# Hard graph attention on one core: a new order on ScalarE and VectorE, one copy of the turned keys, and the normalised rows written by GpSimd

## The chip, the core and the metric

The kernel runs on one core of a Trainium2 chip, as one launch. The metric is the device time in microseconds (us). Its engines are TensorE (PE, with its weight loads PEld), VectorE (DVE), ScalarE (ACT), GpSimd (POOL) and SyncE (SP, which only issues DMAs here). Each engine runs its own list of instructions in order and waits on semaphores that the others raise. ps_... tiles lie in PSUM, the others in SBUF; PE writes into PSUM only.

## The reference

There are 4096 nodes with 256 features, and a random 0/1 matrix adj of 4096 x 4096, dense in its first rows and columns and thinner towards the last ones. For each of 8 heads, only the neighbours with the highest score count, and each with 1/8:

```python
Q, K, V = (x @ WQ.T), (x @ WK.T), (x @ WV.T)          # split into 8 heads of 32
attn = einsum('hqd,hkd->hqk', Q, K) * SCALING + (Q @ we.T + be)
attn = softmax(attn + where(adj > 0, 0.0, -inf))
hard = (attn == max(attn, axis=-1, keepdims=True)) / HEADS
y = layernorm(x + einsum('hqk,hkd->hqd', hard, V), eps=1e-5)
```

## The kernel before, in words

**Prologue.** The projections are made for all nodes. The queries stay in SBUF (q_t); keys and values, the latter in three bf16 parts, go to a table in DRAM (kv_table) of 640 words a row.

**Items.** The queries are taken in groups of 32 (GQ), four groups to a tile of 128 rows, 32 tiles in all. A group needs only the nodes that any of its queries has as a neighbour. Those are gathered 372 at a time (three chunks of 124); such a gather is an *item*. A group has between 1 and 12 items; the run makes some 200. Four items make a *turn* (RING = 4, b = 0 to 3 in the code), and one body for a turn is run in a loop on each engine. SP plans the turns ahead and writes flags for each: fe_on (a new tile of adj is cast and packed), fin_on (its lists are finished), te_on (a tile of results is finished: te_done is its number).

**One item m, engine by engine.** ACT makes `reached` from the ends of the item (owners, line 621). PE multiplies it with the packed lists (planes_of, line 1199). DVE finds the neighbours and their masks from that (pick, line 926: hit, hit_vals, picks, bits). POOL gathers the rows by three indirect DMAs into kv[m % 8] (gather, line 527) and copies the queries (queries, line 522). ACT turns the bits into `masked` (masks, line 654). PE transposes the keys, both halves of four heads, into the two banks of ps_both[m % 2] (keys_across, line 1241), and raises pe_kt[h] for each half; ACT copies each half into k_t (keys, line 660) and raises act_kt[h]. PE makes the scores into the same two banks (scores, line 1215). DVE takes their minimum (tops, line 948: best), then the running minimum (minus_top), and then whether the old one still holds (keep). ACT compares the scores with minus_top (hards, line 664: two instructions). PE transposes the result (hards_across, line 1232), ACT copies it back (hard_rows, line 650: hard_t), PE multiplies with the values into ps_o (values, line 1249), and DVE adds it onto o_all, which is first multiplied by keep (merge, line 962: two instructions).

**The order in a step b.** The engines are in different items at the same time:

- PE: planes_of(b+4), scores(b+1), values(b-1), hards_across(b), keys_across(b+2).
- ACT: masks(b+2), hard_rows(b), owners(b+5), keys(b+2), then hards(b+1). The casts of adj (joined, line 605) stand at b = 0 (quarter 0, behind hards), b = 1 (quarter 1 ahead of hards, 2 behind it) and b = 2 (quarter 3, ahead of hards).
- DVE: pick(b+4), tops(b+1), merge(b-1).
- POOL: queries(b+2), gather(b+3).

PE writes into ps_o for item b only when merge(b-1) has read it, and it writes hard_t's source again only when act_hard has come. scores waits for act_kt[1], the second half alone.

**A finished tile** (te_on). At b = 1 DVE turns o_all (turn_rows, line 972) behind pick and ahead of tops, and PE multiplies it back into ps_y (rows_back, line 1263). At b = 2 DVE adds x and takes mean and variance (norm_stats, line 978) between pick and tops. ACT takes the root (row_std, line 671: std) at b = 2, behind keys and cast_quarter(3) and ahead of hards. DVE then makes rstd and y_out (norm_rows, line 990) behind tops and ahead of merge. SP stores y_out when dve_row is raised (line 479). The last tile is finished after the loop.

The lines that the change and the steps of the prediction touch: 237 to 238 (semaphores of the keys), 475 to 480 (store), 509 to 576 (POOL), 654 to 709 (ACT), 948 to 960 and 990 to 996 and 1099 to 1104 (DVE), 1218 and 1241 to 1247 (PE).

Of the kernel before, what the change touches and what calls it, by code (L numbers as in the profile page):

```python
# [38 lines left out]
def hard_attention(nc, x, adj, wq, wk, wv, we, be, out):  # L39
# [24 lines left out]
    with ExitStack() as ctx:  # L64
# [161 lines left out]
        def item_sem(name, ahead):  # L226
# [10 lines left out]
        pe_kt = [item_sem(f"pe_kt{h}", 2) for h in range(HALVES)]  # L237
        act_kt = [item_sem(f"act_kt{h}", 1) for h in range(HALVES)]
# [6 lines left out]
        dve_turned, pe_y, dve_y, act_std, dve_row = (  # L245
            sem("dve_turned"), sem("pe_y"), sem("dve_y"), sem("act_std"), sem("dve_row"))
# [111 lines left out]
        def _(sp):  # L358
# [116 lines left out]
            def rows(t, row, last):  # L475
# [3 lines left out]
                sp.wait_ge(dve_row, t + 1)  # L479
# [30 lines left out]
        def _(pool):  # L510
# [7 lines left out]
            r = registers(pool, ("n", "left", "g", "next", "more", "due", "at_turn", "col") + tuple(places("q", 1)),  # L518
# [27 lines left out]
            def load_more():  # L546
                at = pool.snap(r["at_turn"], min_val=0, max_val=TURNS - 1)
                pool.reg_load([r["more"]], turn_flags[0:1, bass.ds(at, 1), FLAGS.index("more"):])
# [7 lines left out]
            def turn(first):  # L556
                for b in range(RING):
# [4 lines left out]
                    if b == 2:  # L562
                        plan_made(pool, r)
                        load_places(pool, r, QUERY, places("q", 1))
                        load_more()
                        step()

# [7 lines left out]
            run_turns(pool, r, [lambda: turn(0), lambda: turn(RING)])  # L575
            twice = (pool.snap(r["n"]) - BASE) >> 3
# [6 lines left out]
        def _(act):  # L583
            for s in act_kt + [act_reached, act_masked, act_hard, act_hard_t]:
                act.sem_inc(s, credit(s))
# [74 lines left out]
            def keys(m, due, h):  # L660
                act.wait_ge(pe_kt[h], due(pe_kt[h]))
                act.copy(k_t[m % 2][:, h, :], ps_s[m % 2][h][:, 0:SLOTS]).then_inc(act_kt[h], 1)  # L662
# [13 lines left out]
            for m in range(2):  # L676
                masks(m, for_item(m))
                for h in range(HALVES):
                    keys(m, for_item(m), h)
            hards(0, for_item(0))  # L680

            def turn():
# [4 lines left out]
                for b in range(RING):  # L687
                    masks(b + 2, for_loop(act, r, 2))
                    hard_rows(b, for_loop(act, r, 0))
                    owners(b + 5, for_loop(act, r, 5), f"ahead{b + 5}")  # L690
                    for h in range(HALVES):
                        keys(b + 2, for_loop(act, r, 2), h)
# [5 lines left out]
                    if b == 2:  # L698
                        cast_quarter(3)
                        with rows_due(act, r):  # L700
                            row_std(tile_of(act, r, "te_done"))
                    if b == 3:
                        take_plan()
# [698 lines left out]
```

## Time and profile before

| | us |
|---|---|
| median of 3 runs | 1316.35 (1309.31 to 1316.83) |
| the profiled execution | 1317.37 |
| its span, first to last instruction | 1315.6 |
| of it, the stretch taken as the loop of items in the rows below | 240 to 1310 |

The profiled execution is 1.8 us beyond its span, and 1.0 us above the median. Busy times are of instructions that compute; register work, waits and branches are not busy. The mean granted TensorE clock is 0.918 of full speed.

### The profile page before, as it was taken

The numbers are of one execution on the slowest core, as the hardware profiler recorded it, in microseconds if no ns is written. First come the engines' busy times: TensorE is split into PE (matmuls) and PEld (weight loads), VectorE is DVE, ScalarE is ACT, GpSimd is POOL, SyncE is SP. The second block draws the span as 40 slices with busy tenths as digits, with TensorE's granted clock in tenths as the row PEclk, the third lists the DMA queues.
The fourth block names the chain that finished last, engine by engine and source line by source line (L and its number), as shares of the span: only waits on it lengthen the run. The fifth ranks groups of instructions, "written<-read, shape, count | busy, mean of one in ns | idle before, by whom it ended". The sixth has DMA issues, their size and how long they took to land.

```text
span 1315.6 us, 51593 instructions
## 1 busy us (share of the span) xinstructions
PE 951.6 (72%) x14758; PEld 616.6 (47%) x14759; DVE 929.0 (71%) x2616; ACT 892.0 (68%) x1688; POOL 632.8 (48%) x820
## 2 busy tenths in 40 slices
PE   4787648777777778777787777777777777777771
PEld 2343325454544555455454545455445545455540
DVE  5444536777878777777787777777777777778880
ACT  1523347778777787777877877877777777766770
POOL 0000065675656566555565555554554455445650
PEclk9988877999999998989999899989998989989995
DMA  4634468677687787678777878778878787756770
GB/s 155 214 128 160 145 201 279 196 231 255 197 263 217 243 253 234 215 242 266 248 207 231 268 226 262 252 230 272 257 235 258 248 251 254 254 180 194 212 213 4
DMA packets 89522, 291.06 MB, mean 221 GB/s; under 512 B 16984, under 2 KB 30040, under 8 KB 89496
## 3 DMA queue, kind: packets, MB, share of 16 engines
q0 software_dynamic: 48720, 199.60, 49.5%
q1 hardware_dynamic: 40776, 91.15, 20.4%
q8 instruction: 12, 0.20, 0.1%
q14 instruction: 14, 0.11, 0.0%
HBM read 275.98 MB, written 14.71 MB: 221 GB/s over the span
## 4 chain that ended last, share of the span: by engine, by line
DVE 26%; PE 25%; issue 20%; ACT 15%; DVEq 7%; DMA 3%; ACTq 2%; SPq 1%; POOL 1%; POOLq 0%
DVE best L951 6%; ACT joined L605 5%; PE ps_both L1222 4%; ACT k_t L662 4%; PE ps_both L1154 4%; DVE picks L941 3%; PE ps_h L1237 3%; PE ps_o L1257 3%; DVE hit_vals L934 3%; PE ps_r L1267 3%; DVE hit L928 2%; PE ps_both L1227 2%; ACT hard L667 2%; PE ps_both L1144 2%; DVE o_all L968 2%
## 5 line engine op out<-in xcount | busy, mean ns | idle before, releaser
L532 POOL DMA_INDIRECT kv<-kv_table,picks x309 | 294.9, 954 | 231.3 <-DVE picks L941 127.6
L532 POOL DMA_INDIRECT early<-kv_table,picks x300 | 286.2, 954 | 246.0 <-DVE picks L941 131.6
L652 ACT ACTIVATE hard_t<-ps_h 128x768 bf16<-128x768 bf16 x200 | 162.0, 810 | 233.1 <-PE ps_h L1237 227.4
L667 ACT ACTIVATE hard<-ps_both,minus_top 128x384 bf16<-128x384 f32 x402 | 214.1, 594 | 32.9 <-DVE minus_top L955 30.3
L1222 PE MATMUL ps_both<-k_t,q_now 32*32 32x384 f32 x3216 | 192.6, 534 | 32.1 <-ACT k_t L662 29.0
L951 DVE TENSOR_REDUCE best<-ps_both 128x2 f32<-128x768 f32 x201 | 190.7, 949 | 28.0 <-PE ps_both L1227 17.8
L1207 PE MATMUL ps_x<-pay,reached 128*128 x1224 | 120.2, 233 | 99.6 <-ACT reached L624 93.3
L662 ACT COPY k_t<-ps_both 128x384 f32<-128x384 f32 x404 | 171.6, 479 | 14.4 <-PE ps_both L1245 14.3
L968 DVE SCALAR_TENSOR_TENSOR o_all<-o_all,keep,ps_o 128x96 f32 x400 | 107.7, 311 | 61.8 <-issue 26.5
L1207 PEld LDWEIGHTS ps_x<-pay,reached 128*128 128x128 bf16 x1224 | 83.7, 102 | 137.5 <-ACT reached L624 128.0
L605 ACT ACTIVATE joined<-adj_in,minus_half 128x1024 bf16<-128x1024 int32 x128 | 147.9, 1164 | 0.0
L1227 PEld LDWEIGHTS ps_both<-mask_of,masked 128*128 128x128 bf16 x1206 | 72.9, 102 | 140.9 <-issue 140.9
L525 POOL COPY q_now<-q_t 128x64 f32 x202 | 50.4, 249 | 167.4 <-issue 164.3
L656 ACT ACTIVATE masked<-bits,one 124x384 bf16<-124x384 uint32 x202 | 127.6, 631 | 1.4 <-issue 1.4
L624 ACT ACTIVATE reached<-iota_h,edge_of 128x384 bf16<-128x384 f16 x205 | 124.1, 605 | 1.3 <-DVE pay L906 0.8
L1227 PE MATMUL ps_both<-mask_of,masked 128*128 128x128 bf16 x1206 | 109.4, 231 | 0.0
L1237 PE MATMUL ps_h<-ident_b,hard 128*128 128x128 bf16 x1200 | 107.6, 229 | 0.0
L941 DVE TENSOR_REDUCE picks<-hit_vals 128x9 uint32<-128x288 f32 x204 | 92.7, 455 | 15.1 <-DVE hit_vals L934 9.8
L934 DVE TENSOR_TENSOR hit_vals<-ps_x,hit 128x288 f32<-128x288 f32 x204 | 93.3, 458 | 7.0
L1245 PE MATMUL ps_both<-ident_f,kv 128*128 128x128 f32 x612 | 87.6, 281 | 12.0 <-DMA kv<-kv_table,picks 12.0
L1245 PE MATMUL ps_both<-ident_f,early 128*128 128x128 f32 x600 | 90.5, 291 | 1.6 <-DMA early<-kv_table,picks 1.6
L928 DVE SCALAR_TENSOR_TENSOR hit<-ps_x,slot_of,slot 128x96 f32<-128x96 f32 x204 | 64.0, 314 | 31.5 <-issue 16.1
(145 smaller groups left out, 1309.5 us busy)
## 6 DMA issues: line engine op xcount, KB each, us to landing
adj_in<-in_adj SPq DMA_DIRECT2D x128, 512.0 KB, 5.7
kv_table<-early SPq DMA_DIRECT2D x32, 320.0 KB, 2.4
kv<-kv_table,picks POOLq DMA_INDIRECT x309
early<-kv_table,picks POOLq DMA_INDIRECT x300
early<-in_x SPq DMA_DIRECT2D x8, 512.0 KB, 6.8
x_row<-in_x SPq DMA_DIRECT2D x32, 128.0 KB
out<-y_out SPq DMA_DIRECT2D x32, 128.0 KB
plan<-places_of SPq DMA_DIRECT2D x212, 0.0 KB
```

Source lines behind the costliest of these rows:

```text
L532: pool.indirect_dma_start(kv[m % KVS][:, c, :], None, kv_table, bass.IndirectOffsetOnAxis(ap=picks[m % RING][:, c, 2:3], axis=0)).then_inc ...
L605: act.activation(joined[:, i * QW:(i + 1) * QW], adj_in[:, i * QW:(i + 1) * QW], ACT.Sign, bias=minus_half[:]).then_inc(act_cast, 1)
L652: act.activation(hard_t[m % 2][:], hard_rows_t, ACT.Copy, bias=1.0).then_inc(act_hard_t, 1)
L662: act.copy(k_t[m % 2][:, h, :], ps_s[m % 2][h][:, 0:SLOTS]).then_inc(act_kt[h], 1)
L667: done = act.activation(hard[m % 2][:, h, :], ps_s[m % 2][h][:, 0:SLOTS], ACT.Sign, bias=minus_top[m % 2][:, h:h + 1], scale=-1.0)
L951: dve.tensor_reduce(best[:], ps_both[m % 2][:, :, 0:SLOTS], AX.X, ALU.min).then_inc(dve_best, 1)
L968: done = dve.scalar_tensor_tensor(out=o_run, in0=o_run, scalar=keep[m % RING][:, h:h + 1], in1=ps_o[:, h * width:(h + 1) * width], op0=ALU ...
L1207: mm = pe.matmul(ps_x[:, c * P:(c + 1) * P], reached[m % 2][:, c * P:(c + 1) * P], pay[:].rearrange("p g i v -> p (g i v)") [:, bass.ds(va ...
L1222: pe.matmul(ps_s[m % 2][h][to:to + GQ, 0:SLOTS], q_now[m % RING][head:head + HD, h, :], k_t[m % 2][head:head + HD, h, :], start=True, stop ...
L1227: mm = pe.matmul(bank[:, c * P:(c + 1) * P], masked[m % RING][:, c, :, :].rearrange("p h q -> p (h q)"), mask_of[:], start=False, stop=(c ...
L1237: mm = pe.transpose(hard_rows_t[:, at:at + P], hard[m % 2][:, h, c * P:(c + 1) * P], ident_b[:])
L1245: mm = pe.transpose(ps_s[m % 2][h][:, c * P:(c + 1) * P], kv[m % KVS][:, c, h * P:(h + 1) * P], ident_f[:])
```

## The change

1. ACT, in each step: owners(b+5) now comes first, then masks(b+2), hard_rows(b), keys(b+2). Before it was masks, hard_rows, owners, keys.
2. The keys of both halves are one copy of 128x768 out of both banks, with one semaphore on either side (pe_kt, act_kt) where there were two.
3. ACT, at b = 2: row_std ahead of cast_quarter(3).
4. DVE, tops: keep is worked out first, by comparing max(old, cap) with best (is_le), and so needs no wait for minus_top; then minus_top, with no wait of its own.
5. DVE, at b = 2: merge ahead of norm_rows.
6. y_out is written by POOL (normal_rows) and no more by DVE. POOL does it at b = 3 behind gather, waits there for st_out and for the reciprocal (dve_norm), and raises pool_row, for which the store on SP and the next norm_stats wait. POOL reads one more flag for it (te_on).

```diff
@@ -234,16 +234,15 @@
         q_made = item_sem("q_made", 1)
-        pe_kt = [item_sem(f"pe_kt{h}", 2) for h in range(HALVES)]
-        act_kt = [item_sem(f"act_kt{h}", 1) for h in range(HALVES)]
+        pe_kt, act_kt = item_sem("pe_kt", 2), item_sem("act_kt", 1)
         pe_score = [item_sem(f"pe_score{h}", 1) for h in range(HALVES)]
...
 
-        dve_turned, pe_y, dve_y, act_std, dve_row = (
-            sem("dve_turned"), sem("pe_y"), sem("dve_y"), sem("act_std"), sem("dve_row"))
+        dve_turned, pe_y, dve_y, act_std, pool_row = (
+            sem("dve_turned"), sem("pe_y"), sem("dve_y"), sem("act_std"), sem("pool_row"))
         dve_norm = sem("dve_norm")
@@ -476,7 +475,7 @@
                     sp.dma_start(x_row[:], x[bass.ds(row + P, P), :]).then_inc(ld_row, 16)
-                sp.wait_ge(dve_row, t + 1)
+                sp.wait_ge(pool_row, t + 2)
                 sp.dma_start(out[bass.ds(row, P), :], y_out[:]).then_inc(st_out, 16)
@@ -515,7 +514,8 @@
             pool.sem_inc(q_made, credit(q_made))
-            r = registers(pool, ("n", "left", "g", "next", "more", "due", "at_turn", "col") + tuple(places("q", 1)),
+            pool.sem_inc(pool_row, 1)
+            r = registers(pool, ("n", "left", "g", "next", "more", "due", "at_turn", "col", "te_on", "te_now", "te_done") + tuple(places("q", 1)),
                           n=BASE, left=1, due=PLANNED)
@@ -545,7 +545,13 @@
                 at = pool.snap(r["at_turn"], min_val=0, max_val=TURNS - 1)
-                pool.reg_load([r["more"]], turn_flags[0:1, bass.ds(at, 1), FLAGS.index("more"):])
+                pool.reg_load([r["te_on"], r["more"]], turn_flags[0:1, bass.ds(at, 1), FLAGS.index("te_on"):])
+
+            def normal_rows(te):
+                wait_alone(pool, st_out, te * 16 + 16)
+                wait_alone(pool, dve_norm, te * 4 + 4)
+                pool.tensor_scalar(y_out[:], y[:], mean_var[:, 0:1], rstd[:, 0:1], ALU.subtract, ALU.mult
+                                   ).then_inc(pool_row, 1)
 
@@ -562,8 +568,13 @@
                         load_places(pool, r, QUERY, places("q", 1))
+                        pool.reg_mov(r["te_now"], r["te_on"])
                         load_more()
                         step()
+                    if b == 3:
+                        with pool.If_ne(r["te_now"], 0):
+                            normal_rows(tile_of(pool, r, "te_done"))
+                        pool.reg_add(r["te_done"], r["te_done"], r["te_now"])
 
@@ -573,6 +584,7 @@
             run_turns(pool, r, [lambda: turn(0), lambda: turn(RING)])
+            normal_rows(T - 1)
             twice = (pool.snap(r["n"]) - BASE) >> 3
@@ -581,7 +593,7 @@
         def _(act):
-            for s in act_kt + [act_reached, act_masked, act_hard, act_hard_t]:
+            for s in [act_kt, act_reached, act_masked, act_hard, act_hard_t]:
                 act.sem_inc(s, credit(s))
@@ -657,9 +669,9 @@
 
-            def keys(m, due, h):
-                act.wait_ge(pe_kt[h], due(pe_kt[h]))
-                act.copy(k_t[m % 2][:, h, :], ps_s[m % 2][h][:, 0:SLOTS]).then_inc(act_kt[h], 1)
+            def keys(m, due):
+                act.wait_ge(pe_kt, due(pe_kt))
+                act.copy(k_t[m % 2][:], ps_both[m % 2][:, :, 0:SLOTS]).then_inc(act_kt, 1)
 
@@ -675,8 +687,7 @@
                 masks(m, for_item(m))
-                for h in range(HALVES):
-                    keys(m, for_item(m), h)
+                keys(m, for_item(m))
             hards(0, for_item(0))
@@ -685,20 +696,19 @@
                 for b in range(RING):
+                    owners(b + 5, for_loop(act, r, 5), f"ahead{b + 5}")
                     masks(b + 2, for_loop(act, r, 2))
                     hard_rows(b, for_loop(act, r, 0))
-                    owners(b + 5, for_loop(act, r, 5), f"ahead{b + 5}")
-                    for h in range(HALVES):
-                        keys(b + 2, for_loop(act, r, 2), h)
+                    keys(b + 2, for_loop(act, r, 2))
                     if b == 0:
...
                     if b == 2:
-                        cast_quarter(3)
                         with rows_due(act, r):
                             row_std(tile_of(act, r, "te_done"))
+                        cast_quarter(3)
                     if b == 3:
@@ -952,12 +962,11 @@
                 capped = cap_of[:].rearrange("p g i -> p (g i)")[:, bass.ds(at, 1)]
+                dve.scalar_tensor_tensor(out=keep[m % RING][:], in0=minus_top[(m + 1) % 2][:], scalar=capped,
+                                         in1=best[:], op0=ALU.max, op1=ALU.is_le
+                                         )._wait_ge(dve_best, due(dve_best)).then_inc(dve_keep, 1)
                 dve.scalar_tensor_tensor(out=minus_top[m % 2][:], in0=minus_top[(m + 1) % 2][:], scalar=capped,
-                                         in1=best[:], op0=ALU.max, op1=ALU.min
-                                         )._wait_ge(dve_best, due(dve_best)).then_inc(dve_minus, 1)
-                dve.scalar_tensor_tensor(out=keep[m % RING][:], in0=minus_top[(m + 1) % 2][:], scalar=capped,
-                                         in1=minus_top[m % 2][:], op0=ALU.max, op1=ALU.is_equal
-                                         )._wait_ge(dve_minus, due(dve_minus)).then_inc(dve_keep, 1)
+                                         in1=best[:], op0=ALU.max, op1=ALU.min).then_inc(dve_minus, 1)
 
@@ -978,6 +987,7 @@
                 dve.wait_ge(ld_row, te * 16 + 16)
+                dve.wait_ge(pool_row, te + 1)
                 dve.tensor_tensor(y[:], ps_y, x_row[:], ALU.add).then_inc(dve_y, 1)
@@ -990,10 +1000,6 @@
                 dve.reciprocal(rstd[:], std[:]).then_inc(dve_norm, 2)
-                dve.wait_ge(dve_norm, te * 4 + 4)
-                dve.wait_ge(st_out, te * 16 + 16)
-                dve.tensor_scalar(y_out[:], y[:], mean_var[:, 0:1], rstd[:, 0:1], ALU.subtract, ALU.mult
-                                  ).then_inc(dve_row, 1)
 
@@ -1096,12 +1102,12 @@
                         dve.reg_mov(r["fe_on"], r["fe_next"])
+                    if b > 0 or begun:
+                        merge(b - 1, for_loop(dve, r, -1),
+                              dve.snap(r[f"running{b - 1}" if b else "running_last"], min_val=0, max_val=(2 * GPT - 1) * HALVES * PARTS * HD))
                     if b == 2:
...
                             norm_rows(tile_of(dve, r, "te_done"))
-                    if b > 0 or begun:
-                        merge(b - 1, for_loop(dve, r, -1),
-                              dve.snap(r[f"running{b - 1}" if b else "running_last"], min_val=0, max_val=(2 * GPT - 1) * HALVES * PARTS * HD))
                     dve.reg_add(r["n"], r["n"], 1)
@@ -1115,7 +1121,7 @@
         def _(pe):
-            for s in [pe_planes, pe_hard_t, pe_pv] + pe_kt + pe_score:
+            for s in [pe_planes, pe_hard_t, pe_pv, pe_kt] + pe_score:
                 pe.sem_inc(s, credit(s))
@@ -1215,7 +1221,7 @@
                 pe.wait_ge(q_made, due(q_made))
-                pe.wait_ge(act_kt[1], due(act_kt[1]))
+                pe.wait_ge(act_kt, due(act_kt))
                 for j in range(HEADS4):
@@ -1244,7 +1250,7 @@
                                           kv[m % KVS][:, c, h * P:(h + 1) * P], ident_f[:])
-                    mm.then_inc(pe_kt[h], 1)
+                mm.then_inc(pe_kt, 1)
 
```

## Rows read from the trace of the kernel before

**Rows 1.** The page, part 1: busy us (share of the span) xinstructions

```profile
PE 951.6 (72%) x14758; PEld 616.6 (47%) x14759; DVE 929.0 (71%) x2616; ACT 892.0 (68%) x1688; POOL 632.8 (48%) x820
```

**Rows 2.** Stretches, 240 to 1310: the sum of six

```profile
sum 1070.00, PE 786.12 PEld 526.36 DVE 805.14 ACT 791.77 POOL 588.67; mean PE 131.02 PEld 87.73 DVE 134.19 ACT 131.96 POOL 98.11
```

**Rows 3.** Groups on DVE, 240:1310: line, form, xcount | busy, mean ns | idle <-releasers

```profile
L951 DVE TENSOR_REDUCE best<-ps_both 128x2 f32<-128x768 f32 x190 | 180.2, 948 | 9.0 <-DVE n_items L896 5.6 <-issue 0.9 <-PE ps_both L1227 0.7
...
L955 DVE SCALAR_TENSOR_TENSOR minus_top<-minus_top,cap_of,best 128x2 f32<-128x2 f32 x190 | 42.8, 225 | 6.7
L958 DVE SCALAR_TENSOR_TENSOR keep<-minus_top,cap_of 128x2 f32<-128x2 f32 x191 | 42.1, 221 | 6.7
...
L995 DVE TENSOR_SCALAR y_out<-y,mean_var,rstd 128x256 f32<-128x256 f32 x31 | 13.3, 430 | 4.4
```

**Rows 4.** Waits, 240:1310: who waited for whom, us, times, longest

```profile
ACT hard_t L652 <- PE ps_h L1237: 215.3, 185, 3.0
...
PE ps_x L1207 <- ACT reached L624: 87.3, 121, 1.3
...
DVE rstd L992 <- ACT std L673: 42.5, 25, 3.2
```

**Rows 5.** Timeline, steps with no tile at work: start, us, engine line op

```profile
269.06 0.81 ACT L652 ACTIVATE hard_t<-ps_h 128x768 bf16<-128x768 bf16 x1 [0.86 <-PE ps_h L1237]
...
269.76 0.60 ACT L624 ACTIVATE reached<-iota_h,edge_of 128x384 bf16<-128x384 f16 x1
...
270.27 0.85 ACT L662 COPY k_t<-ps_both 128x384 f32<-128x384 f32 x2
...
271.26 0.88 PE L1222 MATMUL ps_both<-k_t,q_now 32*32 32x384 f32 x16 [0.28 <-ACT k_t L662]
...
272.88 0.51 PE L1237 MATMUL ps_h<-ident_b,hard 128*128 128x128 bf16 x6
...
273.43 0.81 ACT L652 ACTIVATE hard_t<-ps_h 128x768 bf16<-128x768 bf16 x1 [0.86 <-PE ps_h L1237]
```

**Rows 6.** Timeline, step b = 2 of a turn that casts and finishes a tile

```profile
736.11 0.22 DVE L955 SCALAR_TENSOR_TENSOR minus_top<-minus_top,cap_of,best 128x2 f32<-128x2 f32 x1
736.37 0.22 DVE L958 SCALAR_TENSOR_TENSOR keep<-minus_top,cap_of 128x2 f32<-128x2 f32 x1
...
737.11 0.85 ACT L662 COPY k_t<-ps_both 128x384 f32<-128x384 f32 x2
...
737.84 1.17 ACT L605 ACTIVATE joined<-adj_in,minus_half 128x1024 bf16<-128x1024 int32 x1
...
738.89 0.30 ACT L673 ACTIVATE std<-mean_var,eps 128x1 f32<-128x1 f32 x1
```

**Rows 7.** Timeline of DVE, the end of that step

```profile
739.29 0.16 DVE L992 RECIPROCAL rstd<-std 128x1 f32<-128x1 f32 x1 [2.70 <-ACT std L673]
739.60 0.41 DVE L995 TENSOR_SCALAR y_out<-y,mean_var,rstd 128x256 f32<-128x256 f32 x1
739.93 0.54 DVE L968 SCALAR_TENSOR_TENSOR o_all<-o_all,keep,ps_o 128x96 f32 x2
740.38 0.31 DVE L928 SCALAR_TENSOR_TENSOR hit<-ps_x,slot_of,slot 128x96 f32<-128x96 f32 x1
```

**Rows 8.** Timeline, two DVE instructions with no wait between them

```profile
710.13 0.15 DVE L883 COPY ends<-ps_x 128x4 f32<-128x4 f32 x1
710.20 0.15 DVE L884 SCALAR_TENSOR_TENSOR count_f<-ps_x,flag 128x4 f32<-128x4 f32 x1
```

**Rows 9.** Groups on ACT, 0 to the end

```profile
L662 ACT COPY k_t<-ps_both 128x384 f32<-128x384 f32 x404 | 171.6, 479 | 14.4 <-PE ps_both L1245 14.3
L652 ACT ACTIVATE hard_t<-ps_h 128x768 bf16<-128x768 bf16 x200 | 162.0, 810 | 233.1 <-PE ps_h L1237 227.4 <-issue 5.7
```

**Rows 10.** Groups on POOL, 0 to the end

```profile
L532 POOL DMA_INDIRECT kv<-kv_table,picks x309 | 294.9, 954 | 231.3 <-DVE picks L941 127.6 <-issue 70.8 <-PE ps_o L1257 28.6
...
L525 POOL COPY q_now<-q_t 128x64 f32 x202 | 50.4, 249 | 167.4 <-issue 164.3 <-PE ps_both L1227 2.1
```

## Prediction

> **What bounds the kernel now.** I read the shares of the engines first, then the stretches, the groups of DVE, the waits, and last single steps in order of time.
>
> No engine is full over the span: PE 72%, DVE 71%, ACT 68% [rows 1]. In the loop from 240 to 1310 us DVE computes for 805 of 1070 us, 75%, and ACT for 792 [rows 2]. That doesn't look like a bound. But DVE's instructions are short (some 0.2 to 1 us), and between them stand gaps in which no other engine is awaited. The reduction to best, which needs the scores, sat idle for 9.0 us ahead of 190 instructions, and of these only 0.7 us for PE's scores [rows 3]: when DVE gets to the scores they are there. In most steps, so, DVE's own list sets the pace, gaps included, and what is taken out of the list is taken from the time.
>
> One wait on DVE is large: rstd waits 42.5 us for ACT's std, 25 times, up to 3.2 us [rows 4]. The steps show why. The root stands behind a cast of 1.17 us on ACT, and behind the two copies of keys (737.11, 737.84, 738.89) [rows 6]. DVE had started keep at 736.37 and was idle for 2.70 us until 739.29; merge and the next hit, which other engines wait for, stood behind it, at 739.93 and 740.38 [rows 7].
>
> A second ring matters where nothing else is to be done, PE and ACT: hard_t at 269.06, reached, the key copies at 270.27, scores at 271.26, hards_across at 272.88, hard_t again at 273.43, 4.37 us [rows 5]. ACT idles in it before hard_t (215.3 us in the loop), PE before the planes for reached (87.3 us) [rows 4]. It bounds only a few steps early in the loop, for elsewhere an item takes 1070 / 190 = 5.63 us.
>
> **The change, part by part.** All sums are made against the profiled execution, 1317.4 us, which is 1.0 us above the median of the runs.
>
> *keep ahead of minus_top.* Now minus_top starts at 736.11 and keep, which waits for it, at 736.37: 0.26 us [rows 6]. Afterwards minus_top follows keep with no wait. The trace has a pair of small instructions with no wait between them: each takes 0.15 us, and the second starts 0.07 us after the first, an overlap of 0.08 [rows 8]. With keep's 0.22 us [rows 3] that makes 0.22 - 0.08 = 0.14 us, so 0.12 us less on DVE. Some 200 items by 0.12 = 24 us. Bounds: nothing (they start as far apart as now), and 0.19 us if the second starts 0.07 behind whatever the first takes (38 us). I take 24, since the overlap rather than the distance should carry over. Against it, minus_top is ready 0.14 us later for ACT's hards. That costs nothing while ACT gets to hards later than DVE to minus_top; it is 0.14 a step where ACT waits there.
>
> The Trainium skill ("VectorE: DVE Perf Modes", section "The DRAIN you can't avoid") says that the next VectorE instruction does not start until the pipe is empty, and that a semaphore between two costs nothing extra. By that rule this part would give nothing, and the forecast would be higher by the term; the pair of rows above speaks against it.
>
> *y_out to GpSimd.* DVE loses the step from 739.60 to 739.93, 0.33 us, and the one from rstd to y_out, 0.31, is replaced by a start of the next group, some 0.2 [rows 7]. So about 0.43 us a tile, as much as the instruction's own mean of 430 ns [rows 3]; 32 tiles, 14 us. POOL gets a wait and an instruction of 256 elements a row. The nearest row is its copy of 64 elements, 249 ns [rows 10]; at least that, at most four times that, 1.0 us; I take 0.65. Behind it on POOL stand the next queries and gather. That gather needs picks of the item that DVE takes up only after rstd, so the wait for rstd holds nothing up, and POOL has room: it is busy 589 of 1070 us [rows 2], and 32 x 0.65 = 21 us more leave it far from full. The store of the tile and its result buffer come later, with a whole turn to spare. Only behind the last tile is it in the open: 0.2 to 0.6 us. If the cover were gone, the price is the instruction itself, 32 x 0.65 = 21 us.
>
> *std ahead of the cast, merge ahead of rstd.* std was issued 1.05 us behind the cast's start (737.84 to 738.89) [rows 6]; it now takes the cast's place. owners, which took 0.51 us between hard_t and the key copies (269.76 to 270.27) [rows 5], is moved to where ACT idled. So std comes some 1.56 us earlier. DVE gets to rstd later, since merge goes first: 739.93 to 740.38 is 0.45, and some 0.8 us with the gap ahead of it [rows 7]. A wait of up to 2.36 us is gone; of 2.70 some 0.3 is left. Of the 42.5 us [rows 4] I leave 5, for the longest of the 25 waits: 37 us gained. Bounds: 10 us, if the whole chain on ACT is late and the wait only moves, and 42. The cast itself comes 0.3 us later, and so do hards in the step, which stay where they were behind the pair. Late next is ACT: in a turn with four casts it must do 4 x 1.17 us beside its five instructions an item.
>
> *owners first.* The ring loses 0.51. ACT does owners in the time in which it waited for ps_h; if the transposes are there already, hard_t comes up to 0.51 later, but k_t, which follows both, does not. DVE is the bound in most steps, so nearly all of this is slack; I put 4 us for the early steps of 4.37 us.
>
> *One copy of the keys.* The first half no longer starts while PE still turns the second. But hard_t is ahead of it on ACT, and it starts when hards_across is done, as keys_across begins, so both halves are there when ACT comes. The two copies take 0.85 us from start to end [rows 5]; hard_t, with the 768 elements of the new copy, takes 0.81 [rows 9]. 0.04 us an item on ACT, 8 us in all, none of it on DVE's list: 0, within 3 us either way. scores waited for the second half anyway.
>
> *Given back.* At 1070 - 75 = 995 us for 190 items, 5.24 each, ACT would be busy for some 79% and the waits between PE, ACT and DVE, which cost little now, grow. I take 8 us back, a tenth of the gains; nothing in the trace gives it exactly, 0 to 25.
>
> **The sum:** 24 + 14 + 37 + 4 - 8 = 71 us; 1317.4 - 71 = 1246 us.
>
> **The rivals.**
>
> *A. The small instructions do not overlap.* keep and minus_top are as far apart as before. For it: both take a value from SBUF by a pointer, which the pair in the trace that overlaps did not both do. 1246 + 24 = 1270 us.
>
> *B. The wait for std stays, shorter.* ACT, with two casts at b = 1 behind each other, is late as a whole; then moving single instructions gains 10 us rather than 37: 1246 + 27 = 1273 us. For it: DVE, relieved, gets there earlier. Against it: ACT waits 215 us for ps_h, so it catches up in most steps [rows 4]. With A, 1297.
>
> *C. More than the list of DVE.* The ring of PE and ACT bounds more steps than I think, and its 0.55 us tells in a quarter of the 190 items (26 us): 1246 - 22 = 1224 us. For it: PE idles 87 us for reached [rows 4]. Against it: the 9.0 us [rows 3].
>
> *D. Slower than before.* With owners and masks both ahead of hard_rows, hard_t comes 0.51 us later in the steps in which PE is ready; values, and by it merge on DVE, wait for it. This decides if PE's values for the item ahead are already what merge waits for. At 190 steps of 0.51, 97 us, against gains of 75: 1317 + 97 - 75 = 1339 us. Against it: ACT's idle time of 215.3 us in 185 waits is 1.16 us each [rows 4], more than the 0.60 that owners takes [rows 5].
>
> *E. GpSimd in the way.* y_out at 1.0 us or more, in DVE's way or ahead of late gathers, gives back all of its 14 us and its own 32 us: 1246 + 46 = 1292 us. The Trainium skill ("SBUF — State Buffer", section "SBUF: two separate sides") has a DVE instruction with two SBUF inputs and a GpSimd one that reads SBUF shut each other out for the length of the first; no row here shows one beside the other clearly.
>
> **How the numbers follow.** The forecast has 0.50, A 0.14, B 0.12, C 0.13, E 0.05, D 0.03; a whole that changes nothing measurable (A, B and E together) 0.03. A measurement of this kernel can tell about 1% from no change, 13 us, so faster is anything under 1303, which takes in E: 0.94, less 0.02 for causes not thought of, 0.92; within 1%: 0.04; slower, D and half of those causes: 0.04. The range goes from C, 1222, to between B and A with B together, 1286.
>
> **What would show it.** In the profile after: minus_top starts some 0.14 us behind keep, and the waits for keep at merge are gone; rstd's wait falls from 42.5 to some 5 us; no y_out on DVE, and a TENSOR_SCALAR on POOL of 0.4 to 1.0 us; the idle time before hard_t falls by about half; one COPY of 128x768 of 0.81 us an item; best still hardly waits for PE. The forecast is wrong if keep and minus_top are 0.2 us or more apart, if rstd still waits over 15 us, or if best or hit begin to wait for PE by tens of us.

## The result and the profile after

The kernel after took 1254.38 us (median of 4 runs, 1249.99 to 1259.92) against 1316.32 before: a ratio of 0.954, 95% interval 0.949 to 0.959, 62 us less. The forecast was 1246. The profiled execution took 1259.92 us, the highest of the four, with a span of 1258.1 and a mean granted clock of 0.937 (0.918 before), so its rows show 57 us of the gain.

The page's part 1, against [rows 1]:

```profile
PE 926.1 (74%) x14758; PEld 608.3 (48%) x14759; DVE 902.1 (72%) x2584; ACT 885.9 (70%) x1486; POOL 674.2 (54%) x852
```

ACT is nearly as busy as before (885.9 us against 892.0), and the work of DVE fell by 27 us, less than half of the gain: on DVE more than half came out of gaps and waits. The groups of DVE in the loop, 240 to 1250 us, against [rows 3]:

```profile
L961 DVE TENSOR_REDUCE best<-ps_both 128x2 f32<-128x768 f32 x190 | 180.2, 948 | 10.5 <-DVE n_items L906 5.6 <-issue 1.6 <-PE ps_both L1233 1.5
...
L938 DVE SCALAR_TENSOR_TENSOR hit<-ps_x,slot_of,slot 128x96 f32<-128x96 f32 x189 | 59.6, 315 | 46.2 <-PE ps_x L1213 31.1 <-issue 13.0
...
L965 DVE SCALAR_TENSOR_TENSOR keep<-minus_top,cap_of,best 128x2 f32<-128x2 f32 x190 | 42.8, 225 | 6.8
L968 DVE SCALAR_TENSOR_TENSOR minus_top<-minus_top,cap_of,best 128x2 f32<-128x2 f32 x190 | 40.8, 215 | 0.0
...
L916 DVE CAST pay<-ps_x 128x128 f32 x26 | 7.6, 292 | 28.6 <-PE ps_x L1213 25.4 <-issue 3.3
...
L1002 DVE RECIPROCAL rstd<-std 128x1 f32<-128x1 f32 x31 | 5.1, 164 | 3.9 <-ACT std L685 3.4
```

keep now comes first; minus_top has no idle time ahead of it. y_out is gone. rstd's wait for std is 3.4 us, where it was 42.5 [rows 4]. best still hardly waits for PE. But hit waits 31.1 us for PE's planes, and pay (the ranks of the next lists) 25.4 us. Both are answers that DVE awaits from PE. The same waits in the kernel before, with two more that are needed below (merge's for keep, and that of ACT's hards for minus_top):

```profile
DVE hit L928 <- PE ps_x L1207: 7.6, 22, 0.8
...
DVE pay L906 <- PE ps_x L1207: 15.3, 15, 2.0
...
DVE o_all L968 <- DVE keep L958: 22.8, 56, 0.5
...
ACT hard L667 <- DVE minus_top L955: 27.5, 37, 1.5
```

merge's wait for keep is gone from the list after. hit's wait for PE has grown by 23.5 us; the prediction had named this ("if best or hit begin to wait for PE by tens of us") as a sign that it is wrong. The waits of the other engines, against [rows 4]:

```profile
ACT hard_t L664 <- PE ps_h L1243: 89.9, 115, 3.1
ACT hard L679 <- DVE minus_top L968: 71.2, 82, 2.9
...
POOL q_now L525 <- issue: 34.5, 20, 3.6
...
PE ps_both L1251 <- DMA early<-kv_table,picks: 13.7, 12, 2.1
...
PE ps_both L1251 <- DMA kv<-kv_table,picks: 8.3, 9, 2.6
```

ACT's wait for ps_h fell from 215.3 to 89.9 us, and PE's for reached (87.3 us) is gone from the list. ACT's wait for minus_top grew from 27.5 to 71.2 us: ACT now often reaches hards before DVE has minus_top. New are 34.5 us of GpSimd ahead of q_now with no engine named (0.8 before), and 22 us of PE waiting for gathered keys (2.2 before). These two were not in the forecast.

The end of a step b = 2, to be held against [rows 6] and [rows 7]:

```profile
895.82 0.29 ACT L685 ACTIVATE std<-mean_var,eps 128x1 f32<-128x1 f32 x1
...
896.25 1.15 ACT L617 ACTIVATE joined<-adj_in,minus_half 128x1024 bf16<-128x1024 int32 x1
...
896.77 0.22 DVE L965 SCALAR_TENSOR_TENSOR keep<-minus_top,cap_of,best 128x2 f32<-128x2 f32 x1
...
896.91 0.21 DVE L968 SCALAR_TENSOR_TENSOR minus_top<-minus_top,cap_of,best 128x2 f32<-128x2 f32 x1
897.12 0.54 DVE L977 SCALAR_TENSOR_TENSOR o_all<-o_all,keep,ps_o 128x96 f32 x2
...
897.67 0.16 DVE L1002 RECIPROCAL rstd<-std 128x1 f32<-128x1 f32 x1
...
898.62 1.24 POOL L553 TENSOR_SCALAR y_out<-y,mean_var,rstd 128x256 f32<-128x256 f32 x1
```

minus_top starts 0.14 us behind keep, std stands ahead of the cast, o_all comes straight behind minus_top, and rstd behind it waits for nothing. y_out starts on GpSimd 0.95 us later and takes 1.24 us.

### The profile page after: what moved, and what is told of

It is laid out like the page before. It is cut to its first block, busy times and chain, and to the rows that moved or that the text cites. A ratio compares the mean times of both kernels' runs of the same rounds, so it can differ in the third digit from the quotient of the medians.

```text
span 1258.1 us, 51532 instructions
## 1 busy us (share of the span) xinstructions
PE 926.1 (74%) x14758; PEld 608.3 (48%) x14759; DVE 902.1 (72%) x2584; ACT 885.9 (70%) x1486; POOL 674.2 (54%) x852
## 3 DMA queue, kind: packets, MB, share of 16 engines
q0 software_dynamic: 48720, 199.60, 51.5%
## 4 chain that ended last, share of the span: by engine, by line
DVE 31%; PE 19%; issue 18%; DMA 10%; ACT 7%; DVEq 7%; POOL 3%; SPq 1%; POOLq 1%; ACTq 1%
DVE best L961 7%; DVE picks L951 5%; DMA early<-kv_table,picks 4%; PE ps_both L1160 4%; PE ps_r L1273 4%; DVE hit_vals L944 4%; DVE hit L938 3%; DMA kv<-kv_table,picks 3%; ACT joined L617 3%; PE ps_both L1150 2%; PE ps_both L1251 2%; POOL kv L532 2%; DMA be_sb<-in_L_gnn_be 2%; ACT hard_t L664 1%; DVE o_all L977 1%
## 5 line engine op out<-in xcount | busy, mean ns | idle before, releaser
L1228 PE MATMUL ps_both<-k_t,q_now 32*32 32x384 f32 x3216 | 183.8, 512 | 55.0 <-ACT k_t L674 53.3
L674 ACT COPY k_t<-ps_both 128x768 f32<-128x768 f32 x202 | 161.2, 798 | 39.4 <-PE ps_both L1251 39.0
L1213 PE MATMUL ps_x<-pay,reached 128*128 x1224 | 115.7, 226 | 40.2 <-issue 32.9
L1233 PEld LDWEIGHTS ps_both<-mask_of,masked 128*128 128x128 bf16 x1206 | 69.9, 99 | 132.7 <-issue 132.7
L636 ACT ACTIVATE reached<-iota_h,edge_of 128x384 bf16<-128x384 f16 x205 | 126.9, 619 | 2.9 <-issue 1.6
L668 ACT ACTIVATE masked<-bits,one 124x384 bf16<-124x384 uint32 x202 | 124.5, 616 | 0.0
L1243 PE MATMUL ps_h<-ident_b,hard 128*128 128x128 bf16 x1200 | 103.7, 224 | 6.7 <-ACT hard L679 4.7
L1251 PE MATMUL ps_both<-ident_f,kv 128*128 128x128 f32 x612 | 90.3, 286 | 20.6 <-DMA kv<-kv_table,picks 20.2
L1233 PE MATMUL ps_both<-mask_of,masked 128*128 128x128 bf16 x1206 | 105.0, 225 | 0.0
L1251 PE MATMUL ps_both<-ident_f,early 128*128 128x128 f32 x600 | 84.4, 276 | 14.2 <-DMA early<-kv_table,picks 13.7
```

The source lines that it names most:

```text
L674: act.copy(k_t[m % 2][:], ps_both[m % 2][:, :, 0:SLOTS]).then_inc(act_kt, 1)
L1213: mm = pe.matmul(ps_x[:, c * P:(c + 1) * P], reached[m % 2][:, c * P:(c + 1) * P], pay[:].rearrange("p g i v -> p (g i v)") [:, bass.ds(va ...
L1228: pe.matmul(ps_s[m % 2][h][to:to + GQ, 0:SLOTS], q_now[m % RING][head:head + HD, h, :], k_t[m % 2][head:head + HD, h, :], start=True, stop ...
L1233: mm = pe.matmul(bank[:, c * P:(c + 1) * P], masked[m % RING][:, c, :, :].rearrange("p h q -> p (h q)"), mask_of[:], start=False, stop=(c ...
L1251: mm = pe.transpose(ps_s[m % 2][h][:, c * P:(c + 1) * P], kv[m % KVS][:, c, h * P:(h + 1) * P], ident_f[:])
```

## The experiments

Each was timed beside the kernel before on the same chip. Its median was 1315.88 us beside keep_alone, undo_std, rows_on_dve and plan_first, and 1316.33 us, on a second chip, beside undo_keep, undo_owners, two_copies and dve_plan_first; so the medians of these eight and of the kernel after (1316.32 beside it) can be compared. The intervals of the ratios leave 3 to 7 us of uncertainty to each. The edits are shown in short form, with arguments and some names cut ("..."); the full lines of the change stand in its diff.

**keep_alone**: part 4 alone, in the kernel before.

```diff
+keep = (max(old, cap) <= best)._wait_ge(dve_best)
-minus_top = min(max(old, cap), best)._wait_ge(dve_best)
-keep = (max(old, cap) == minus_top)._wait_ge(dve_minus)
+minus_top = min(max(old, cap), best)
```

> The kernel before with part 4 alone (keep first, minus_top with no wait). By the forecast's term, 0.12 us less on VectorE's list in each of some 200 items: 24 us, about 1293 us. By what the trace after shows (from the first of the two to the start of merge 0.28 us less where nothing else holds it), up to 50 us, less what the wait for std takes back in 12 turns that cast and finish a tile (there it grows by what VectorE gains ahead of it): 30 to 40 us, 1276 to 1286. If the two small instructions did not overlap, no gain.

Measured: 1297.50 us, ratio 0.985 (0.981 to 0.988), 18 us less; the forecast's 24 was nearer than the 30 to 40 expected here. The wait for std grew, from 42.5 us to

```profile
DVE rstd L991 <- ACT std L673: 49.2, 24, 3.6
```

which is what the expectation had as the mechanism. But these 7 us do not explain a gain that is 12 us or more short; hit's wait for PE's planes grew as well, from 7.6 to 26.9 us. By kinds of turns (the table in the next section) the 12 turns that pack lists took 232.5 us in place of 243.1, and the 12 that cast and finish a tile gained nothing (278.2 against 274.9).

**undo_keep**: part 4 undone in the kernel after (the diff above, backwards).

> The kernel after with part 4 undone (minus_top first, keep waits for it). Alone on the kernel before this part gained 18 us, and the wait for std grew by 7 us beside it. If that wait took back what the part gave, then here, where the wait for std is gone, the part is worth more: 30 to 45 us above the kernel after. If the part is worth the same wherever it stands: 18 us above.

Measured: 1278.33 us, ratio 0.971 (0.967 to 0.974), 24 us above the kernel after. This lies between the two expectations, and closer to the lower one; with the uncertainty of the medians neither is excluded. The part is worth some 20 us in either kernel, the size that the forecast worked out. A step of its trace, with nothing else between the three instructions:

```profile
273.23 0.22 DVE L965 SCALAR_TENSOR_TENSOR minus_top<-minus_top,cap_of,best 128x2 f32<-128x2 f32 x1
273.48 0.22 DVE L968 SCALAR_TENSOR_TENSOR keep<-minus_top,cap_of 128x2 f32<-128x2 f32 x1
273.81 0.54 DVE L978 SCALAR_TENSOR_TENSOR o_all<-o_all,keep,ps_o 128x96 f32 x2
```

From the first of the pair to merge it is 0.58 us here and 0.35 in the kernel after (896.77 to 897.12 above).

**undo_std**: parts 3 and 5 undone in the kernel after.

```diff
+cast_quarter(3)
 with rows_due(act, r): row_std(...)
-cast_quarter(3)
...
-merge(b - 1, ...)
 with rows_due(dve, r): norm_rows(...)
+merge(b - 1, ...)
```

> The kernel after with parts 3 and 5 undone: the root behind the cast, rstd ahead of merge. If that pair carries what the forecast gave it, 37 us, this kernel takes 25 to 40 us more than the one after, and rstd's wait is back at 30 to 50 us. If owners first alone would have brought std early enough, 10 to 15 us more.

Measured: 1271.19 us, ratio 0.966 (0.962 to 0.969), 17 us above the kernel after: between the two. Of the wait for std only half is back:

```profile
DVE rstd L1002 <- ACT std L685: 23.2, 13, 2.1
```

So something else in the change had halved it. That is owners:

**undo_owners**: part 1 undone in the kernel after.

```diff
-owners(b + 5, ...)
 masks(b + 2, ...)
 hard_rows(b, ...)
+owners(b + 5, ...)
```

> The kernel after with part 1 undone: masks, hard_rows, owners on ScalarE. If the loop of PE and ScalarE (4.37 us before, of which owners is 0.51) would now bound the plain steps of 3.6 us, and PE waits for reached again, 15 to 40 us more than the kernel after. If it is slack as the forecast had it: 4 us, not to be told from none.

Measured: 1278.69 us, ratio 0.971 (0.968 to 0.975), 24 us above the kernel after. The forecast's 4 us are refuted. The wait for reached, which owners first had removed, is back, and with it part of that for std:

```profile
PE ps_x L1213 <- ACT reached L636: 83.5, 118, 1.3
...
DVE rstd L1002 <- ACT std L685: 17.6, 12, 1.9
```

The granted clock was 0.913 to 0.925 in its four executions, against 0.937 to 0.941 in those of the kernel after. So PE also ran at its higher clock for more of the time with owners first; how much of the 24 us is that, and how much the waits, was not separated.

**two_copies**: part 2 undone in the kernel after.

```diff
-act.wait_ge(pe_kt, ...); act.copy(k_t[m % 2][:], ps_both[m % 2][:, :, 0:SLOTS])
+for h in range(HALVES):
+    act.wait_ge(pe_kt[h], ...); act.copy(k_t[m % 2][:, h, :], ps_s[m % 2][h][:, 0:SLOTS])
```

> The kernel after with part 2 undone: two copies of the keys, two semaphores on each side. Forecast: 0 within 3 us either way. Rival: where the gathered keys come late, the first copy runs beside the second half's transposes, and two copies are faster by up to 0.4 us in some 30 items, 5 to 10 us.

Measured: 1251.48 us, ratio 0.950 (0.948 to 0.952) against 0.954 (0.949 to 0.959): no difference that can be told.

**rows_on_dve**: part 6 undone in the kernel after; y_out is made by DVE behind the reciprocal, which comes behind merge.

```diff
 dve.reciprocal(rstd[:], std[:]).then_inc(dve_norm, 2)
+dve.wait_ge(dve_norm, te * 4 + 4)
+dve.wait_ge(st_out, te * 16 + 16)
+dve.tensor_scalar(y_out[:], y[:], ...).then_inc(pool_row, 1)
...
-normal_rows(...)      # on GpSimd
```

> The kernel after with y_out on VectorE again, behind the reciprocal. Theory 1 (SyncE waits for the late pool_row ahead of the next plan, and GpSimd for the plan): the move to GpSimd gained 0.43 us x 31 on VectorE but cost about as much or more in late gathers, so this kernel takes the same as the one after or up to 8 us less; the waits of PE for gathered keys fall from some 30 us to under 8 us, and GpSimd's wait ahead of q_now (34.5 us) is gone. Rival (the late gathers come from the faster pace and the fuller DMA queues): the waits for gathered keys stay, and the time is 13 us higher.

Measured: 1243.37 us, ratio 0.944 (0.942 to 0.946), 11 us *less* than the kernel after, somewhat beyond the 8 us of theory 1. The move to GpSimd was a loss. The waits fell, but not as far as expected: PE's for gathered keys to 13.1 us (expected under 8), GpSimd's ahead of q_now to 11.0 us (expected gone).

**plan_first**: y_out stays on GpSimd; on SyncE the next turn's plan is issued ahead of the finished tile's store and of the load of the next x_row.

```diff
-with sp.If_ne(r["te_on_was"], 0): rows(...)
+sp.reg_mov(r["rows_on"], r["te_on_was"]); sp.reg_mov(r["rows_of"], r["te_was"])
 plan_next()
 sp.reg_add(r["n"], r["n"], RING)
+with sp.If_ne(r["rows_on"], 0): rows(...)
```

> The kernel after, with the store of the tile and the load of the next x_row put behind the next turn's plan on SyncE. Theory 1: GpSimd no longer waits for the plan, the stray long steps of the last turns and of the turns before 850 us go, 10 to 17 us less than the kernel after. Rival (fuller DMA queues, or GpSimd's 1.23 us itself): within 3 us of the kernel after, and the waits for gathered keys stay near 30 us.

Measured: 1244.25 us, ratio 0.945 (0.943 to 0.948), 10 us less than the kernel after, without taking the work from GpSimd. The rival (GpSimd's 1.23 us itself, or fuller DMA queues) falls: the instruction still takes 1233 ns, and the packets of the gathers take 51.8% of the DMA engines' time in place of 51.5% (the page, part 3). How the loss came about is seen in the last turns of the kernel after. First GpSimd, then SyncE, in order of time:

```profile
1170.42 0.95 POOL L532 DMA_INDIRECT kv<-kv_table,picks  x1 [0.30 <-issue]
1174.97 0.23 POOL L525 COPY q_now<-q_t 128x64 f32 x1 [3.60 <-issue]
...
1178.53 0.95 POOL L532 DMA_INDIRECT kv<-kv_table,picks  x1 [0.30 <-issue]
1179.60 1.24 POOL L553 TENSOR_SCALAR y_out<-y,mean_var,rstd 128x256 f32<-128x256 f32 x1
```

```profile
1159.88 0.36 SPq L479 DMA_DIRECT2D out<-y_out  x1
1161.94 7.28 SPq L401 DMA_DIRECT2D plan<-places_of  x4
1170.27 0.65 SPq L426 DMA_DIRECT2D turn_flags<-flags_of  x1
...
1181.01 0.36 SPq L479 DMA_DIRECT2D out<-y_out  x1
1183.08 0.71 SPq L401 DMA_DIRECT2D plan<-places_of  x1
```

The store at 1181.01 waits for y_out, which ends at 1180.84; only 2.07 us behind the store come the next turn's plans (1183.08). The turn before shows what that does: store at 1159.88, four plans from 1161.94 on, the flags at 1170.27. GpSimd can't go beyond b = 2 of its turn before the plan and the flags have landed: it stands idle for 3.60 us ahead of q_now at 1174.97. Behind that stand the gathers, behind them the next y_out, and behind that again the store and the plan. And PE is without its keys:

```profile
1182.83 1.54 PE L1251 MATMUL ps_both<-ident_f,kv 128*128 128x128 f32 x6 [2.63 <-DMA kv<-kv_table,picks]
```

SyncE's waits at the store, first in the kernel after, then in the kernel before:

```profile
SPq L479 <- POOL y_out L553: 52.0, 20, 7.7
```

```profile
SPq L480 <- DVE y_out L995: 13.0, 5, 3.1
```

In plan_first the idle time ahead of q_now is 2.2 us in place of 34.5, and PE's waits for gathered keys are 13.5 us in place of 22.0:

```profile
PE ps_both L1253 <- DMA early<-kv_table,picks: 8.1, 10, 1.8
...
PE ps_both L1253 <- DMA kv<-kv_table,picks: 5.4, 9, 1.2
...
POOL q_now L527 <- issue: 2.2, 4, 0.7
```

**dve_plan_first**: both repairs together.

> Both repairs together: y_out on VectorE and the plan ahead of the store. If both repairs act through the plan on SyncE alone, the second adds nothing to the first: 1243 within 4 us. If the early plan is worth something by itself also with an early y_out: 1236 to 1239.

Measured: 1248.24 us, ratio 0.948 (0.946 to 0.950). Nothing was added, which fits two repairs that act through the same place; but it came out 5 us above rows_on_dve, just outside the 4 us expected, and that is not explained. (Its profiled execution took 1257.40 us, 9 above its median; where that one lost is said under "Given back".)

**On a third chip: owners_alone, std_alone, owners_std, dve_two.** These were to give the parts by themselves in the kernel before, and the four good parts (1, 3, 4, 5) together. owners_alone has part 1 in the kernel before, std_alone parts 3 and 5, owners_std parts 1, 3 and 5; dve_two is rows_on_dve with two_copies.

> The kernel before with part 1 alone (owners first on ScalarE). Undone in the kernel after it cost 24 us, of which about half stood in the step b = 2 of the 12 turns that cast and finish a tile, where std came 0.5 us earlier or more, and the rest in steps that PE and ScalarE bound. In the kernel before VectorE's list is longer, and only the first of these counts in full: 8 to 15 us. If it is worth the same everywhere: 24 us. If std's wait is not eased by it: 4 us, as the forecast had it.

> The kernel before with parts 3 and 5 alone (root ahead of the cast, merge ahead of rstd). The forecast gave the pair with owners first 37 us; undone in the kernel after it cost 17 us. Here the wait of 42.5 us is whole: 15 to 25 us, and a wait of 5 to 15 us left for std. If it needs owners first: under 12 us.

> The kernel before with parts 1, 3 and 5 together: the wait for std should be under 8 us. If both act through that wait they overlap: 25 to 35 us less than before, under the sum of the two alone. If each acts in a place of its own: the sum of the two.

> The kernel after with y_out on VectorE and two copies of the keys: parts 1, 3, 4 and 5 of the change alone. y_out on VectorE gained 11 us on the kernel after, two copies 3 us in the middle and nothing surely. If the two add: 1240 us; if the second is none: 1243. Rival: two copies lose what they save on ScalarE, 1247.

They decided none of this. On this chip the granted TensorE clock was far lower, and the kernel before took 1769.33 us (1751.95 to 1797.05 in 17 executions, clock 0.77 to 0.78). The rows of cores, in the order owners_alone, owners_std, dve_two, std_alone:

```profile
core 0: 1671.7 us, clock 0.799
```

```profile
core 0: 1695.9 us, clock 0.793
```

```profile
core 0: 1761.2 us, clock 0.768
```

```profile
core 0: 1858.1 us, clock 0.760
```

Measured: owners_alone 1669.29 us, ratio 0.941 (0.932 to 0.950); owners_std 1684.28, 0.951 (0.943 to 0.960); dve_two 1783.46, 1.007 (1.001 to 1.012); std_alone 1858.74 (1815 to 1890), for which there is no ratio. No expectation was met. The executions of one kernel lie 1.5 to 4% apart, so most of these differences are those of the kernels and not chance; and the times, that of the kernel before among them, stand in the order of the granted clocks. Read as effects of the edits they would say that part 4 alone costs 99 us here, for dve_two and owners_std differ by nothing else, where it gained 18 and 24 us above; and that parts 3 and 5 alone cost 89. Whether an edit changes the clock and by it the time, or the clock follows from something else, isn't shown. I draw nothing from them about what the parts are worth on the other chips.

## Why the prediction was right or wrong

The sign and the size were right, 71 us forecast and 62 measured, for reasons that were partly other ones. The table has the time from the first hit of a turn to the first of the next, taken from the starts of hit in each trace and summed over the turns of one kind (us, one profiled execution each). Three turns are left out, the first two and the only one that packs lists and finishes a tile without casting; the last turn is counted up to its last hit:

| | 5 plain turns | 12 that pack lists | 12 that cast and finish a tile | 14 that do all | last 4 |
|---|---|---|---|---|---|
| before | 84.1 | 243.1 | 274.9 | 351.0 | 72.5 |
| after | 78.3 | 232.8 | 242.8 | 337.9 | 76.3 |
| keep_alone | 85.3 | 232.5 | 278.2 | 347.6 | 70.0 |
| undo_keep | 81.2 | 244.2 | 243.5 | 340.7 | 76.9 |
| undo_owners | 83.9 | 234.3 | 254.8 | 335.3 | 76.6 |
| undo_std | 77.8 | 233.3 | 258.5 | 336.8 | 76.8 |
| rows_on_dve | 77.4 | 232.6 | 242.8 | 335.7 | 69.1 |
| plan_first | 78.0 | 232.4 | 242.2 | 333.2 | 68.0 |

- **"DVE's own list sets the pace"**, in most steps: right for the 12 turns that pack lists, and not for most steps. In these 12, undo_keep gave back the part almost exactly (243.1, 232.8, 244.2), and no other row of the kernel after with one part undone moves them by more than 1.5 us. But of the 12 that cast and finish a tile it moved only 0.7 us (242.8 to 243.5), where 48 steps at the 0.12 us of the forecast would be 5.8; of the 14 that do all, 2.8 us in place of 6.7. And rows_on_dve puts y_out back on DVE's list in the casting turns and takes the same 242.8 us. So in these 26 turns, once the change is made, DVE's list alone does not set the pace; hit's 31.1 and pay's 25.4 us of waiting for PE say the same.
- **keep ahead of minus_top, 24 us**: right in distance (0.14 us forecast, 0.14 shown) and in size (24 us undone, 18 alone), but the size is in part luck. The distance explains 0.12 us a step. The bare steps of the trace lost some 0.2 to 0.25 us (b = 0 of plain turns 3.83 to 3.62, and 3.87 with the part undone): the other half is merge, which starts 0.33 us behind keep where it waits for keep's result and 0.21 us behind minus_top where keep is made first. So a step gained twice what the forecast gave it, but in fewer than half of the steps. The Trainium skill ("VectorE: DVE Perf Modes", section "The DRAIN you can't avoid") has the next VectorE instruction wait until the pipe is empty, with a semaphore between two at no extra cost; the same section lets an instruction that is not held start earlier. By the first half alone the part would have made nothing; the 0.26 us that became 0.14 and the runs fit the second half. Rival A falls.
- **std ahead of the cast with merge first, 37 us**: the wait went as forecast (42.5 to 3.4 us), but the cause was mis-assigned. Of its 1.56 us I had worked out 0.51 from owners and yet put the whole into this term. Undone, the pair costs 17 us, and owners' share of the same turns costs 12 (242.8 against 254.8). In the 12 turns the whole change gained 32 us (274.9 to 242.8), of which these 15.7 and owners' 12 are the larger part. Rival B (the wait only shorter) falls.
- **owners first, 4 us**: wrong, 24 us. Two steps failed. Some 12 us are the earlier std above, which the forecast had put into the term before: the two terms together were forecast at 41 us and, undone one by one, come to 17 + 24 = 41. And "it bounds only a few steps early in the loop" was too little: in the plain turns the steps b = 1 and 2 stand at 4.31 us with owners undone (the forecast's ring had 4.37) and at 3.81 and 3.58 in the kernel after (medians). That makes 6 us in the five plain turns, and 4 more lie in the first two turns of the loop; the rest are small differences. What the clock does in this is open, as said. Rival C named 22 us for more steps bound by the ring; the number is near, but half of it came by std, and the forecast lost as much in other places, so its time did not come.
- **y_out to GpSimd, 14 us gained**: wrong in sign, 11 us lost. Two steps failed. "The store of the tile and its result buffer come later, with a whole turn to spare": the store had the turn, but the plans behind it in SyncE's queue had not, and plan_first shows that this is where the loss sat. And the price: y_out took 1.23 us on GpSimd, 2.9 times DVE's 0.42 and beyond my bound of 1.0. With the plan repaired the move gains nothing either (1244.25 against 1243.37): on the last tile all of it lies open, and from std to the end takes 6.8 us where it took 3.3 (below), and in the 12 casting turns the step b = 2 is shorter (median 5.45 us in plan_first, 5.86 in rows_on_dve) but b = 1 and b = 3 are longer (5.60 and 5.28 against 5.20 and 5.15), with sums of 242.2 and 242.8. GpSimd's instruction in plan_first:

```profile
L555 POOL TENSOR_SCALAR y_out<-y,mean_var,rstd 128x256 f32<-128x256 f32 x32 | 39.5, 1233 | 36.6 <-DVE rstd L1004 32.7
```

The end of the last tile in the kernel after, then in rows_on_dve:

```profile
1251.33 0.29 ACT L685 ACTIVATE std<-mean_var,eps 128x1 f32<-128x1 f32 x1 [29.96 <-DVE mean_var L998]
...
1252.06 1.22 POOL L553 TENSOR_SCALAR y_out<-y,mean_var,rstd 128x256 f32<-128x256 f32 x1 [28.74 <-DVE rstd L1002]
1254.83 0.36 SPq L479 DMA_DIRECT2D out<-y_out  x1
```

```profile
1239.83 0.29 ACT L679 ACTIVATE std<-mean_var,eps 128x1 f32<-128x1 f32 x1 [29.90 <-DVE mean_var L991]
...
1240.43 0.41 DVE L998 TENSOR_SCALAR y_out<-y,mean_var,rstd 128x256 f32<-128x256 f32 x1
1240.94 0.36 SPq L479 DMA_DIRECT2D out<-y_out  x1
```

The spans end at 1258.1 and 1243.1.

- **One copy of the keys, 0**: right, 3 us that can't be told from none.
- **Given back, 8 us**: the place wasn't named and should have been. In the 14 turns that do all, the step b = 1 stayed at 7.91 us at best, as before, although DVE's list in it had become shorter: DVE turns the tile, PE multiplies it back, then makes the ranks and the planes, and DVE waits for these. In 9 of the 14 (5 before) the step took over 8.5 us. A short such step in the kernel after (its 7.92 us begin with the hit at 708.84), then a long one, with the rows of PE and then DVE:

```profile
713.54 1.60 PE L1273 MATMUL ps_r<-ident,o_t 128*128 128x128 f32 x12 [0.87 <-DVE o_t L983]
...
888.12 2.56 PE L1273 MATMUL ps_r<-ident,o_t 128*128 128x128 f32 x12 [2.38 <-DVE o_t L983]
...
892.15 0.29 DVE L916 CAST pay<-ps_x 128x128 f32 x1 [2.33 <-PE ps_x L1213]
```

pay waits for PE 2.33 us here, and 25.4 us in the loop against 15.3 before. The twelve matmuls took 2.56 us, where they take 1.60 in the short step; the granted clock was at the lower of its two levels (1.2 GHz in place of 2.4) for 3.4 us from 888.5 on, after PE had waited 2.38 us for o_t. The long step and the slow matmuls go together in all ten traces of this kind (before, after and the eight runs): every step of 7.9 to 8.2 us has the twelve matmuls in 1.6 us, and all but one of those over 8.5 have them in 1.7 to 2.9 us, with the clock at its lower level beside them. How often it happens goes from 5 of 14 (before, keep_alone, undo_keep) over 6 to 8 (plan_first, undo_owners, undo_std, rows_on_dve, two_copies) to 9 in the kernel after and 13 in the profiled execution of dve_plan_first. So it isn't simply the faster pace that brings it, for plan_first and rows_on_dve are faster and have 6 and 7. PE's wait of over 2 us stands ahead of each long step of the kernel after, but ahead of some short ones too; what decides between them stays open.

- **D** (slower, by a late hard_t) had no sign: ACT's idle time ahead of hard_t stayed positive, 89.9 us. **E** had y_out's length (over 1.0 us) and late gathers right, but the gathers were late for another reason: not a GpSimd in VectorE's way or its 1.23 us, but a queue behind it.

The parts undone one by one add up to 24 + 24 + 17 - 11 - 3 = 51 us, of the 62 that all make together, within what five medians leave open. So 71 against 62 is also a sum of errors of both signs: y_out missed by 25 us, and the other parts with what is given back, forecast at 57, made the 62 and the 11 that y_out lost. The range's lower end should have been rival C's own 1224, not 1222.

## What to carry to other kernels

Before a piece of work moves to an idle engine, follow the queue of whoever waits for its result, and ask what stands behind that wait: here a store on SyncE held back the plans that the idle engine itself needed. A comparison against an operand's own inputs (is_le against best in place of is_equal against the new minimum) can take a semaphore out of a chain of tiny instructions; here it was worth a quarter of a microsecond a step, and some 20 us of the possible 50 over 200 items, for it tells only in the steps in which that engine's list sets the pace. Busy shares don't say which steps these are; undoing one part and comparing the turns by kind does. The best version measured is the change without its move to GpSimd: 1243.37 us, ratio 0.944, from which plan_first (1244.25) can't be told.

## What was not expected of the hardware

- GpSimd took 1233 ns for 128x256 with two operands by pointer, against 242 ns for its copy of 128x64 and 422 ns for the same instruction on DVE. The Trainium skill ("GPSIMD Engine Reference", section "When to use GPSIMD") has two-input work about twice as slow on GpSimd and one-input work near line rate; with one tensor and two pointers it was 2.9 times here. The 1233 ns are the profile's; in the last turns above, the next instruction on GpSimd starts 1.18 us behind it.
- On the third chip the granted clock was 0.75 to 0.80 in place of 0.91 to 0.95, the kernel before took 34% longer, and the four good parts together gained nothing there (1.007), though three of them without part 4 gained 5% (0.951). The kernel after itself was not run on it; that the gain of this change holds only where PE gets its clock is a guess from one chip.
